# Moving layer 1's bias row from TensorE's matmuls to GpSimd in a two-layer graph attention kernel

## What is computed

```python
q = x @ Wq[k].T + bq[k];  kk = x @ Wk[k].T + bk[k]
scores = where(adj == 0, -1e10, q @ kk.T / sqrt(128))
attn = where(adj == 0, 0, softmax(scores))
x = layer_norm(x + (attn @ x) @ Wc[k].T, ln_g[k], ln_b[k])
```

## Time and profile before

| | |
|---|---|
| median of 3 runs | 1194.66 us (1193.97 to 1195.53) |
| the profiled execution | 1193.67 us |
| its span | 1191.8 us |
| PE busy | 1151.6 us, 97% of the span |
| DVE busy | 975.9 us, 82% |
| ACT busy | 927.7 us, 78% |
| POOL busy | 543.1 us, 46% |
| mean granted TensorE clock | 0.992 |
| DMA | 112.48 MB, mean 94 GB/s |

### The profile page before, as it was taken

The page is one execution under the profiler, slowest core; times in us unless marked ns, Lnnn a source line. Parts: engine busy times, 40 slices in busy tenths (PEclk is TensorE's granted clock), DMA queues, the critical chain, the costliest instruction groups (busy, mean ns, idle before and its releaser), DMA issues.

```text
span 1191.8 us, 28469 instructions
## 1 busy us (share of the span) xinstructions
PE 1151.6 (97%) x9596; PEld 840.7 (71%) x9596; DVE 975.9 (82%) x2680; ACT 927.7 (78%) x2115; POOL 543.1 (46%) x410
## 2 busy tenths in 40 slices
PE   7988999999999999999999999999999999999796
PEld 4656777777777777777777777777777777777463
DVE  5877888898888888888888888888888888888776
ACT  5436888878888787888878888887888888788774
POOL 2561346434544644354454435545443564444330
PEclk9899999999999999999999999999999999999999
DMA  8024261614425152431615234260532516122411
GB/s 230 19 77 102 70 144 37 180 35 125 90 70 162 37 152 63 121 93 47 185 35 145 72 88 126 37 196 19 142 90 72 143 37 182 32 74 74 113 27 36
DMA packets 164446, 112.48 MB, mean 94 GB/s; under 512 B 100944, under 2 KB 146000, under 8 KB 164304
## 3 DMA queue, kind: packets, MB, share of 16 engines
q1 hardware_dynamic: 162144, 102.80, 33.6%
q0 software_dynamic: 2160, 7.87, 1.9%
HBM read 61.87 MB, written 25.17 MB: 73 GB/s over the span
## 4 chain that ended last, share of the span: by engine, by line
PE 90%; DVE 5%; ACT 2%; issue 2%; DMA 1%; POOL 1%; DVEq 0%; POOLq 0%; ACTq 0%; SPq 0%
PE ps_j L868 40%; PE ps_t L881 23%; PE ps_j L1008 10%; PE ps_s L860 8%; PE ps_s L854 7%; ACT probs L1068 1%; PE ps_j L1016 1%; DVE masked_s L1169 1%; DMA xt<-ys 1%; PE ps_j L975 1%; DVE y_l L1288 0%; POOL ys L674 0%; DMA x<-x_dram 0%; DVE stats_L L1189 0%; PE ps_j L1034 0%
## 5 line engine op out<-in xcount | busy, mean ns | idle before, releaser
L1169 DVE CUSTOM_DVE_ANT_0 masked_s<-ps_s,mask 128x512 f32<-128x512 f32 x640 | 424.8, 681 | 21.8 <-PE ps_s L860 21.6
L1068 ACT ACTIVATE probs<-masked_s,nm_h 128x512 f32<-128x512 f32 x512 | 367.3, 718 | 73.3 <-DVE nm_h L1169 66.8
L881 PE MATMUL ps_t<-ident,probs 128*128 128x128 f32 x2560 | 390.5, 275 | 6.7 <-ACT pt_h L1074 3.0
L881 PEld LDWEIGHTS ps_t<-ident,probs 128*128 128x128 f32 x2560 | 305.5, 142 | 86.8 <-issue 23.2
L1074 ACT ACTIVATE pt_h<-ps_t 128x512 f32<-128x512 f32 x401 | 236.2, 589 | 77.3 <-PE ps_t L881 72.5
L860 PE MATMUL ps_s<-stack 128*128 128x512 f16 x512 | 194.5, 381 | 2.6 <-DVE nm_h L1169 2.6
L868 PE MATMUL ps_j<-xw,pt_l 128*128 128x256 f16 x1536 | 189.1, 274 | 1.8 <-DVE parts L1347 1.0
L868 PEld LDWEIGHTS ps_j<-xw,pt_l 128*128 128x128 f16 x1536 | 150.8, 98 | 32.9 <-DVE pt_l L1204 2.1
L656 POOL TENSOR_TENSOR rstd_L<-var_eps_L,minus_half 128x4 f32<-128x4 f32 x32 | 32.8, 1025 | 220.8 <-DVE var_eps_L L1199 220.8
L1008 PE MATMUL ps_j<-pt_h,v 128*32 128x256 f32 x2048 | 123.6, 382 | 2.7 <-DVE pt_h L1176 2.4
L1204 DVE TENSOR_TENSOR pt_l<-ps_t,pt_l 128x512 f16<-128x512 f32 x128 | 88.3, 690 | 30.1 <-ACT pt_l L1074 20.8
(11 more groups left out here) (143 smaller groups left out, 1640.0 us busy)
## 6 DMA issues: line engine op xcount, KB each, us to landing
stack<-bounce SPq DMA_DIRECT2D x256, 128.0 KB, 3.0
bounce<-parts SPq DMA_DIRECT2D x64, 256.0 KB, 2.6
adj_t<-adj_dram SPq DMA_DIRECT2D x30, 512.0 KB, 5.4
x<-x_dram SPq DMA_DIRECT2D x16, 512.0 KB, 3.9
out_dram<-y_f POOLq DMA_DIRECT2D x15, 512.0 KB, 3.4
stack<-adj_dram SPq DMA_DIRECT2D x2, 512.0 KB, 5.7
pt_h<-l_wc SPq DMA_DIRECT2D x2, 256.0 KB, 4.8
out_dram<-y_f SPq DMA_DIRECT2D x4, 128.0 KB, 1.8
```

What stands on the lines that cost most here:

```text
L881: last = pe.transpose(ps_t[r % 2][:, t], probs[:, r, t * P:(t + 1) * P], ident[:])
L1068: act.activation(probs[:, r], masked_s[:, r], ACT.Exp, bias=nm[:, n, r:r + 1], scale=-1.0, accum_out=total[:, n, r:r + 1]).then_inc(exps, 1)
L1169: dve.tensor_tensor_reduce(out=masked_s[:, r], in0=ps_s[scores_bank(pos)][:], in1=m[:, r], scale=-scale, scalar=NONE_LEFT, op0=ALU.add, op ...
```

## The change

The four extra matmuls of XW of layer 1 and `mean_64` go. `bx1` becomes a full fp32 row on all partitions, copied by one DVE operation. At layer 0, DVE makes one more small reduction: `has_l`, the smaller of the row's softmax sum and 1, which is 1 for a row with a neighbour. GpSimd makes `spread` = (bx1 + 0) * has_l with four operations of 128x256, and adds it to `x1` with one of 128x1024, in a new function `add_bx`. `x1` is announced (`ln_done`) only then. The scratch `spread` is `y_l` in the loop and `y_f` for graphs 0 and 1. In the loop body `add_bx` stands behind the split of head outputs 1 and the split of x, and these two change places. The places of the masks in the table of jobs stay. 

```diff
-        bx1 = sb("bx1", [P, D], fp16)
-        mean_64 = sb("mean_64", [P, P], fp16)
+        bx1 = sb("bx1", [P, D])
...
-                pool.tensor_tensor(dst[:], dst[:], h, ALU.add).then_inc(ln_done[s], 1)
+                pool.tensor_tensor(dst[:], dst[:], h, ALU.add).then_inc(shifted if norm == 0 else ln_done[s], 1)
...
+            def add_bx(b, dst):
+
+                if early(b, 1):
+                    pool.wait_ge(bias_ready, 1)
+                    settle(pool)
+                pool.wait_ge(shifted, b + 1)
+                spread = (y_f if early(b, 2) else y_l)[:]
+                for t in range(NT):
+                    last = pool.tensor_scalar(spread[:, t], bx1[:], zero[:], has_l[:, b % 2, t:t + 1], ALU.add, ALU.mult)
+                last.then_inc(bx_spread, 1)
+                pool.wait_ge(bx_spread, b + 1)
+                last = pool.tensor_tensor(dst[:], dst[:], spread, ALU.add)
+                last.then_inc(ln_done["L"], 1)
...
             gain_and_shift("L", nth(0, 0), y_l, 0, x1)
+            add_bx(0, x1)
+            pool.wait_ge(ln_done["L"], 1)
             low_weights(2, 0)
...
             split_x(2)
+            add_bx(1, x1)
...
                 split_o(i, 0)
                 layer_norm_l0(i + 2, 0, x1)
+                split_o(i, 1)
                 split_x(i + 3)
-                split_o(i, 1)
+                add_bx(i + 2, x1)
                 finish(i)
...
                         last = split_product(out_bank[:, t * D:(t + 1) * D], lambda a, c: xt[:, l_buffer(b, l), a, c, at:at + P],
-                                             lambda a, c: wc0[:, a, l, c], more=l == 1)
-                        if l == 1:
-                            last = pe.matmul(out_bank[:, t * D:(t + 1) * D], mean_64[:], bx1[:],
-                                             start=False, stop=True)
+                                             lambda a, c: wc0[:, a, l, c])
...
-                    dve.tensor_scalar(bx1[:], wide[:, 0:D], UP, None, ALU.mult).then_inc(bx1_hi, 1)
...
+                    dve.tensor_copy(bx1[:], wide[:, 0:D]).then_inc(bias_ready, 1)
...
+                        if l == 0:
+                            dve.tensor_reduce(has_l[:, b % 2], sum_l[:, sums_buffer(b, l), :, 0:3:2], ALONG, ALU.min)
+                        dve.tensor_reduce(some_l[:], sum_l[:, sums_buffer(b, l), :, 0:2], ALONG, ALU.max).then_inc(some_ready, 1)
```

More of the change, by code:

```diff
@@ L194, in graph_attention @@
         nm_h = sb("nm_h", [P, H, NT])
-        sum_l = sb("sum_l", [P, 2, NT, 2])
+        sum_l = sb("sum_l", [P, 2, NT, 3])
         sum_h = sb("sum_h", [P, H, NT])
         some_l = sb("some_l", [P, NT])
+        has_l = sb("has_l", [P, 2, NT])
+        zero = sb("zero", [P, 1])
         r_l = sb("r_l", [P, NT])
@@ L232, in graph_attention @@
         ident_zero, ident_in, half_in = sem("ident_zero"), sem("ident_in"), sem("half_in")
-        mean_in, bo_added, bx1_hi = sem("mean_in"), sem("bo_added"), sem("bx1_hi")
+        bo_added, shifted, bx_spread = sem("bo_added"), sem("shifted"), sem("bx_spread")
         pt_lo_ready, xw_hi = sem("pt_lo_ready"), sem("xw_hi")
@@ L645, in _ @@
             pool.memset(sum_l[:, :, :, 1:2], SUM_FLOOR).then_inc(floors_in, 1)
+            pool.memset(zero[:], 0.0).then_inc(floors_in, 1)
+            pool.memset(sum_l[:, :, :, 2:3], 1.0).then_inc(floors_in, 1)
             for s in "LF":
                 pool.memset(moments[s][:, :, 2:3], LN_EPS).then_inc(floors_in, 1)
-            pool.memset(mean_64[:], 1.0 / 64).then_inc(mean_in, 1)
             pool.wait_ge(ident_zero, 1)
@@ L780, in _ @@
             pool.tensor_tensor(x1[:], y_f[:], shift[:, 0:1, :].to_broadcast([P, NT, D]), ALU.add)\
-                .then_inc(ln_done["L"], 1)
+                .then_inc(shifted, 1)
             pool.tensor_tensor(x2[:], y_l[:], gain[:, 1:2, :].to_broadcast([P, NT, D]), ALU.mult)\
@@ L801, in _ @@
             split_o(LOOPS - 1, 1)
+            add_bx(LOOPS + 1, x1)
             finish(LOOPS - 1)
@@ L967, in job @@
                     if early(b, 1) and l == 1:
-                        pe.wait_ge(bias_ready, 1)
                         pe.wait_ge(low_weights_ready, 1)
@@ L1054, in _ @@
             pe.wait_ge(ident_in, 1)
-            pe.wait_ge(mean_in, 1)
             program(walk)
@@ L1321, in job @@
                         if early(L, 1):
-                            dve.wait_ge(floors_in, 3)
-                        dve.tensor_reduce(some_l[:], sum_l[:, sums_buffer(b, l)], ALONG, ALU.max).then_inc(some_ready, 1)
+                            dve.wait_ge(floors_in, 5)
+                        if l == 0:
+                            dve.tensor_reduce(has_l[:, b % 2], sum_l[:, sums_buffer(b, l), :, 0:3:2], ALONG, ALU.min)
+                        dve.tensor_reduce(some_l[:], sum_l[:, sums_buffer(b, l), :, 0:2], ALONG, ALU.max).then_inc(some_ready, 1)
                         dve.wait_ge(some_ready, L + 1)
```

## The result

| | before | changed |
|---|---|---|
| median | 1194.32 us (4 runs, 1193.65 to 1195.53) | 1216.07 us (4 runs, 1214.99 to 1217.09) |
| ratio | | 1.0182 [1.017, 1.0194] |
| the profiled execution | 1193.67 us | 1217.09 us |
| its span | 1191.8 us | 1215.1 us |
| one loop body | 70.31 us | 72.03 us |

What follows compares the result with a forecast made beforehand. PE was taken to bound the kernel, busy 97% of the span. Thirteen bodies at 0.73 us (+9.5) less 0.6 for the last body and prologue gave +8.9, about 1203.6 us; range 1188 to 1208.

Steps and rivals of the forecast that it cites:

- What is added on POOL: Four scalar operations (2.16 us) and an addition (2.37 us) a graph, 4.6 us with the semaphore, costing no time.
- What is moved: On POOL, head outputs are split first; the split of x ends at 591.93 instead of 586.95, at no cost.
- What that meets: DVE's two masks in a body wait for POOL's split of x and addition, making DVE 1.68 us late.
- How PE feels it: PE waits about 1.2 us at tile 38's transposes for tile 36's low half; a body costs 0.73 us more.
- What is removed: 64 PE matmuls at 0.11 us: 0.44 us a body, 0.2 us in the prologue, 6.4 us gained.
- Rival 1: The masks' meetings with POOL don't happen or cost less than DVE's room; the gain arrives, 1188.3 us; chance 0.18.
- Rival 3: POOL keeps its ports through all four scalar operations; the first mask is 2.42 us late, 1213.2 us; chance 0.08.
- Rival 4: POOL starts its scalar operations only at the first mask's end; DVE 1.83 us late, 1205.5 us; chance 0.15.
- the pairs of about 1.0 and 2.1 us: Sign in the profile: the bodies' 26 DVE mask operations take about 1.0 and 2.1 us instead of 0.69.
- PE idle once in each body, ended by the low half: Sign on PE: about a microsecond idle once a body, ended by DVE's low half of an L tile.
- 71.0 us: Sign in the loop: the body's period is 71.0 us instead of 70.3.

## Why the prediction was wrong

The sign, the place and the mechanism of the collision were right; the path by which PE feels it was not, and the time was 12.5 us too low and outside the range. By the steps of the prediction:

- **What is added on POOL**: 2.20 us unhindered, with the masks early, for the four scalar operations (forecast 2.16) and 2.36 for the addition (2.37). Right. In the prologue the first `add_bx` cost nothing that shows; the reader of the second starts at 98.05 against 97.81.
- **What is moved**: right, except that POOL took up the head outputs' split 0.27 us behind the end of their operation (597.23 against 596.27 + 0.69) and not 0.09 behind it. All that follows is 0.18 us later, and so the first mask 0.49 late instead of 0.30. The terms as the prediction gives them add up to 591.99 for the end of the split of x, not 591.93; the 0.06 between them is an overlap that this trace shows too, since POOL's row behind the head outputs' split starts at 599.02 and that ends at 599.08.
- **What that meets**: right nearly to the hundredth. The masks end 0.55 us behind POOL's instructions (forecast 0.54, from the earlier trace rows), they take 1.17 and 2.08 us, and the four scalar operations were held up 0.41 to 0.45 (forecast 0.44, from the earlier trace rows). DVE was 1.88 us late instead of 1.68, most of it the 0.18 above. POOL's scalar operations ended at 604.87 and have 2.20 us of their own, so POOL went on at about 602.67, an estimate from these rows, 0.16 us ahead of the mask's recorded end. On the point where row and page differed, this trace sides with the row. By the Trainium skill (SBUF — State Buffer, "A bandwidth-pool intuition that's wrong"), which has its about 115 ns behind DVE's end from DMA descriptors that GpSimd writes, POOL would go on at 602.83 + 0.115 = 602.95 and end at 605.15, an estimate from the page's figure.
- **How PE feels it**: this step failed. It said that the first thing late is the transposes of tile 38, with 0.58 us of room and 0.43 more on DVE, and a body 0.73 us longer. Two readers of DVE's work come earlier and have less room: the scores of tile 39, with 0.30 us, and those of position 41, with 0.12. The prediction had followed the PSUM buffers of the transposes, which turn regularly, and not those of the scores, whose turn is cut short at just this place. By the same working, with DVE 1.68 us late, they give 1.68 - 0.12 = 1.56 us a body, 13 x 1.56 - 0.6 = +19.7, 1214.4 us. So of the 12.5 us missed, 10.8 are this step and the rest mostly the 0.18. Moving the short turn away took back 10.5 us and left the gap at tile 38 that the step had described.
- **What is removed**: wrong as well, though with next to no effect on the sum, since the gap swallowed it. PE's 0.44 us of a body were counted as gained on the ground that PE is busy all the time. The 0.2 us of the prologue don't show in the profiled execution. With the masks at tiles 29 and 32 only 0.10 arrive, because DVE has 0.12 us in hand at position 41. *Rival 1* would therefore not have given 1188.3 us, but about 1193.
- *Rival 3* had 1213.2 us, near the measured 1216.07, by a mechanism that did not happen: its first mask would have taken 3.1 us, its gap would have stood at tile 33 or 34, and the halves ruled it out. *Rival 4* needed POOL to begin at the mask's end at the earliest; by its durations it began 0.16 us before.

Of the marks named in advance, the pairs of about 1.0 and 2.1 us were there; "PE idle once in each body, ended by the low half" and "71.0 us" were not, and they point to the step that failed.

## What to carry to other kernels

Idle time of an engine is cover only if no other engine has work in it that its instructions hold up: POOL's 11.76 us of idle time were just where DVE's mask operations lay, and 0.69 us of DVE there became 2.08. When an engine gets late, list every reader of every buffer that it releases and take the room of each, irregular turns of a rotation first; PE, busy all the time, had 0.12 us of room towards DVE here, and 0.30 in another place. And before such work is given up, move the operation that it collides with or cut the other engine's instruction in two: here the same work went from 1216 to 1188 and 1203 us.

## What the runs showed of the hardware

- A waiting DVE operation gets in between two POOL instructions that follow each other without a semaphore: with the addition in halves (1.27 us for a half that no mask holds up) the mask took 0.99 instead of 2.08 us. It was the size of POOL's single instruction that counted, not POOL's busy time, which grew.
- A small DVE operation waits as a large one does. One of 128x4 took 0.17 us all 17 times that it met none of POOL's instructions in the kernel before, and 0.60 beside POOL's copy. Once it began 0.07 us ahead of the copy (824.25 against 824.32) and took 0.17. In the changed kernel it took 0.84 us beside the copy that runs from 624.95 to 625.98:

```profile
625.17 0.84 DVE L1214 TENSOR_SCALAR minus_mean_L<-moments_L 128x4 f32<-128x4 f32 x1
```

- The custom masking operations, which read their scores from PSUM, are not touched, as forecast: the 640 of them average 681 ns in both kernels.
